# Router choices by a maximum and index of eight, and first-stage scatters issued in two groups

## The reference

```python
x = x + 0.5 * ffn(layernorm(x))       # 16 experts, the best 2 of each token
x = x + attn(layernorm(x))            # 16 heads, 4 key/value heads, causal
x = x + 0.5 * ffn(layernorm(x))

def ffn(x):
    probs = softmax(x @ router_w)                    # 256 x 16
    routing_weights, routing_idx = top_k(probs, 2)
    routing_weights /= sum(routing_weights)
    # every chosen expert: silu(x @ gate) * (x @ up) @ down, summed with the weights
```

## Time and profile before

| what | us |
|---|---|
| median of 3 runs (858.55 to 863.77) | 861.68 |
| span of the profiled execution | 874.5 |
| the profiled execution's own time | not given apart from its span |
| pool 0 and 1 routed, experts of pool 0 begin | 39.6 |
| experts of pool 1 begin | 87.3 |
| attention runs at PE's pace from about | 222 |

### The profile page before, as it was taken

How to read it: one execution, slowest core, us unless ns; L and a number is a source line. 1 busy time by engine, 2 the same in 40 slices (tenths; PEclk the granted TensorE clock), 3 DMA queues, 4 the chain that set the end, 5 groups by cost and what they waited for, 6 DMA issues and landing times.

```text
span 874.5 us, 16309 instructions
## 1 busy us (share of the span) xinstructions
PE 778.9 (89%) x4584; PEld 667.8 (76%) x4584; DVE 656.2 (75%) x1823; ACT 582.4 (67%) x1538; POOL 451.7 (52%) x410
## 2 busy tenths in 40 slices
PE   3678999899999999999999999999988887899980
PEld 3567878678778888888888887888877777787770
DVE  6645575568988888889988889987899877675463
ACT  2335666687777878877878787787765665554540
POOL 1466232488465866575656655455442782003354
PEclk9789899999999999999999999999999999999995
DMA  9478983212000110000000000000000165256675
GB/s 296 131 213 272 246 243 119 82 22 31 1 1 8 18 19 7 1 13 13 2 13 13 1 1 1 1 2 1 8 0 1 43 220 168 79 160 195 204 210 180
DMA packets 53207, 70.91 MB, mean 81 GB/s; under 512 B 7296, under 2 KB 44928, under 8 KB 52736
## 3 DMA queue, kind: packets, MB, share of 16 engines
q1 hardware_dynamic: 41024, 47.80, 18.1%
q0 software_dynamic: 9216, 16.82, 7.8%
q10 hardware_dynamic: 2880, 5.24, 2.0%
HBM read 42.80 MB, written 27.03 MB: 80 GB/s over the span
## 4 chain that ended last, share of the span: by engine, by line
PE 59%; issue 12%; POOL 11%; DVE 10%; DMA 3%; ACT 2%; SPq 1%; POOLq 0%; DVEq 0%; ACTq 0%
PE ps L1694 49%; PE ps L1891 5%; POOL sb_ropeB L1639 2%; POOL sb_xf L1642 2%; PE ps L1749 2%; POOL xs L1608 1%; POOL sb_x L1630 1%; POOL sb_wF L1650 1%; POOL xs L1601 1%; DVE sb_x L1488 1%; PE ps L1763 1%; DMA xs<-sb_rowC,sb_toC 1%; PE ps L1711 1%; DVE sb_prob L1461 1%; DMA sb_work<-xs 1%
## 5 line engine op out<-in xcount | busy, mean ns | idle before, releaser
L1694 PE MATMUL ps<-sb_wF 128*128 128x512 f32 (+2 forms) x1056 | 262.0, 375 | 9.3 <-DVE sb_wF L1478 6.8
L1694 PEld LDWEIGHTS ps<-sb_wF 128*128 128x128 f32 x1056 | 173.4, 191 | 28.6 <-issue 8.7
L1020 ACT ACTIVATE sb_prob<-sb_prob,sb_nmax 128x128 f32<-128x128 f32 (+3 forms) x256 | 142.2, 559 | 43.8 <-DVE sb_nmax L1461 40.3
L1639 POOL TENSOR_TENSOR sb_ropeB<-sb_ropeB,sb_sin 128x512 f32<-128x512 f32 x80 | 110.9, 1386 | 106.5 <-ACT sb_ropeB L1001 106.4
L1694 PE MATMUL ps<-sb_wF,sb_wA 128*128 128x512 f32 x576 | 154.9, 404 | 6.3 <-ACT sb_ropeB L1001 5.7
L1650 POOL TENSOR_TENSOR sb_wF<-sb_xf,sb_wF 128x384 fp32r<-128x384 f32 (+1 forms) x75 | 82.0, 1101 | 121.0 <-ACT sb_wF L1013 120.8
L1488 DVE SCALAR_TENSOR_TENSOR sb_x<-ps,sb_rinv,sb_x 128x256 f32<-128x256 f32 x256 | 122.5, 479 | 23.3 <-PE ps L1694 9.8
L1694 PEld LDWEIGHTS ps<-sb_wF,sb_wA 128*128 128x128 f32 x576 | 102.2, 188 | 32.0 <-ACT sb_ropeB L1001 13.1
L1694 PE MATMUL ps<-sb_wA,sb_wF 128*128 128x256 f32 x768 | 116.1, 287 | 10.0 <-DVE sb_x L1488 7.1
L1468 DVE TENSOR_TENSOR sb_wF<-ps,sb_wF 128x512 fp32r<-128x512 f32 x160 | 109.2, 684 | 19.7 <-ACT sb_wF L1029 17.1
L1029 ACT ACTIVATE sb_wF<-ps 128x512 fp32r<-128x512 f32 x160 | 95.3, 596 | 42.9 <-PE ps L1891 42.3
(11 more groups left out here) (203 smaller groups left out, 1320.7 us busy)
## 6 DMA issues: line engine op xcount, KB each, us to landing
ys<-sb_wA_raw SPq DMA_DIRECT2D x124, 128.0 KB
sb_wF_raw<-xs SPq DMA_DIRECT2D x44, 128.5 KB
sb_wA_raw<-xs SPq DMA_DIRECT2D x44, 128.5 KB
sb_work<-xs SPq DMA_DIRECT2D x36, 128.5 KB
sb_wA_raw<-in_wattn ACTq DMA_DIRECT2D x18, 256.0 KB, 3.4
sb_wF_raw<-in_wgu SPq DMA_DIRECT2D x4, 768.0 KB
sb_wF_raw<-in_wdn SPq DMA_DIRECT2D x4, 768.0 KB
sb_wA_raw<-in_wgu SPq DMA_DIRECT2D x4, 768.0 KB
```

Of the source, the lines that this page charges most:

```text
L1020: nc.scalar.activation(own, own, ACT.Exp, scale=-1.0, bias=nmax[:, k % 2, h:h + 1], accum_out=ssum[:, k % 2, h:h + 1]).then_inc(exp_done, 1)
L1639: nc.gpsimd.tensor_tensor(ropeB[:, slot], ropeB[:, slot], sin[:], ALU.mult).then_inc(rope_mul, 1)
L1694: return nc.tensor.matmul(out, lhsT, rhs, start=start, stop=stop)
```

## The change

Four things change. **The choice of experts:** for each row of tokens one maximum-of-eight instruction gives the eight largest logits and one index-of-eight instruction their positions, so the two chosen experts and the gap are read off. For the two pools of the first mixture and for the last pool both read the logits in PSUM, and their copy to SBUF falls away; pool 2 still copies. A pool of 12 rows thus has 24 small instructions; two comparisons then make the tables of the choices, laid out expert by expert where they were row by row. In pool 1 the logits of the first 8 rows are in another bank than those of the last 4, and the first 8 are searched by themselves, then the last 4. **Rows 8 to 11 of pool 1** are normalised by VectorE, not ACT. **The first mixture's scatters** go out as all the firsts of a pool, then in two halves one copy of weights and that half's seconds (`scatter_parts`); the wait for pool 0's results is gone. **Pool 1's tables and gather places** are made in five pieces in steps 3, 5, 7, 9 and 11 of pool 0's experts, not two in steps 2 and 4.

```diff
+    FIRST_HALVES, ACT_ROWS = 4, 8
...
-    LEAD, PACED = 9, 13
...
         lx_copy(pools[1], 0)
         for j in (4, 5):
             normalise(pools[1], j)
-        for h in range(1, pools[1].nh):
+        lx_copy(pools[1], 1)
+        for j in (6, 7):
+            normalise(pools[1], j)
+        for h in range(2, pools[1].nh):
             lx_copy(pools[1], h)
-            for j in range(2 * h + 4, min(2 * h + 6, pools[1].nt)):
-                normalise(pools[1], j)
...
-        def pick_top(q, m):
-            link(nc.vector.tensor_reduce(per_token(q, "lm", m), plane(q, 0), AX_X, ALU.max))
-            link(nc.vector.tensor_tensor(plane(q, 1), plane(q, 0), over_e(q, per_token(q, "lm", m)), ALU.is_ge))
-
-        def pick_first(q):
-            rev = falling(q).rearrange("p (o e) -> p o e", o=1).broadcast_to([P, plane(q, 1).shape[1], E])
-            link(nc.vector.tensor_tensor(plane(q, 1), plane(q, 1), rev, ALU.mult))
-            link(nc.vector.tensor_reduce(per_token(q, "lm", 2), plane(q, 1), AX_X, ALU.max))
-
-        def pick_out(q, k):
-            link(nc.vector.tensor_tensor(plane(q, 2 + k), plane(q, 1), over_e(q, per_token(q, "lm", 2)), ALU.is_ge))
...
+        def find_top(q, first, last):
+
+            if q.p == 2:
+                dve.wait_ge(lcopy_done, copies(q, last // 2 - 1))
+            else:
+                dve.wait_ge(logit_done, q.halves + (last // 2 if q.p == 1 else q.nh))
+            for t in range(first, last):
+                step(nc.vector.max(top_value(q, t), logit_row(q, t)))
+            settle()
+            for t in range(first, last):
+                ins = nc.vector.max_index(top_index(q, t), top_value(q, t), logit_row(q, t))
...
+        def pick(q, k):
+
+            a = rising(q).rearrange("p (e o) -> p e o", o=1).broadcast_to([P, E, q.nt])
+            b = index_of(q, k).rearrange("p (o t) -> p o t", o=1).broadcast_to([P, E, q.nt])
+            step(nc.vector.tensor_tensor(plane(q, 2 + k), a, b, ALU.is_equal))
...
-                if q.p == 0 and i in (2, 4):
-
-                    places(pools[1], 3 + (i == 4))
+                if q.p == 0 and i in (3, 5, 7):
+                    tables(pools[1], (i - 3) // 2)
+                elif q.p == 0 and i in (9, 11):
+                    move(pools[1], (i - 9) // 2)
...
-        lcopy(pools[0], 0)
-        for part in range(7):
-            if part == 3:
-                second_norm()
+        route(pools[0], 0)
+        route(pools[0], 1)
+        route(pools[0], 3)
+        second_norm()
+        for part in (4, 5, 6):
             route(pools[0], part)
         shares(pools[0])
-        for part in range(5):
+        for part in range(3):
             places(pools[0], part)
-        lcopy(pools[1], 0)
-        for part in range(7):
+        rows(pools[1], ACT_ROWS, pools[1].nt)
+        for part in (3, 4):
+            places(pools[0], part)
+        find_top(pools[1], 0, 2 * FIRST_HALVES)
+        find_top(pools[1], 2 * FIRST_HALVES, pools[1].nt)
+        for part in (3, 4, 5, 6):
             route(pools[1], part)
...
-            if q.p == 1 and 2 * n > LEAD:
-
-                pool.wait_ge(y_evac, min(2 * n - LEAD, PACED))
...
+        def scatter_parts(q):
+
+            parts = (range(0, q.nt // 2), range(q.nt // 2, q.nt))
+            pool.wait_ge(to_done, q.p + 1)
+            pool.wait_ge(weight_done, q.p + 1)
+            for part, rows in enumerate(parts):
+                for t in rows:
...
+                    nc.gpsimd.indirect_dma_start(out=xs[q.p][:], out_offset=place_of(q, 0, t), in_=rows_of(q)[:, t],
+                                                 in_offset=None).then_inc(first_in[2 * q.p + part], 16)
+            for part, rows in enumerate(parts):
+                pool.wait_ge(first_in[2 * q.p + part], 16 * len(rows))
+                own = slice(rows.start, rows.stop)
+                nc.gpsimd.tensor_copy(row_weights(q)[:, own], wgt[:, q.t0 + rows.start:q.t0 + rows.stop]).then_inc(second_set, 1)
+                pool.wait_ge(second_set, 2 * q.p + part + 1)
+                for t in rows:
+                    nc.gpsimd.indirect_dma_start(out=xs[q.p][:], out_offset=place_of(q, 1, t), in_=rows_of(q)[:, t],
+                                                 in_offset=None).then_inc(scattered[q.p], 16)
...
         for q in pools[0:2]:
-            for n in range(q.nt + SECOND):
-                scatter(q, n)
+            scatter_parts(q)
```

More of the change, by code:

```diff
@@ L10 @@
 I32 = mybir.dt.int32
+U32 = mybir.dt.uint32
 ALU = mybir.AluOpType
@@ L170, in program @@
     RING, XR, FR, GR = 8, 10, 4, 16
+    PART_ROWS = [q.nt // 2 for q in pools[0:2] for _ in range(2)]
     w_in = [sem(f"w_in{n}") for n in range(2)]
@@ L1170, in pick_first @@
-        def pick_first(q):
-            rev = falling(q).rearrange("p (o e) -> p o e", o=1).broadcast_to([P, plane(q, 1).shape[1], E])
-            link(nc.vector.tensor_tensor(plane(q, 1), plane(q, 1), rev, ALU.mult))
-            link(nc.vector.tensor_reduce(per_token(q, "lm", 2), plane(q, 1), AX_X, ALU.max))
-        def pick_out(q, k):
-            link(nc.vector.tensor_tensor(plane(q, 2 + k), plane(q, 1), over_e(q, per_token(q, "lm", 2)), ALU.is_ge))
-        def route(q, part):
-            if part == 0:
-                dve.wait_ge(lcopy_done, copies(q, span(q)[1] // 2 - 1))
-                dve.wait_ge(cf_in, 16 * (1 if q.p < 2 else q.p))
[L1183 to L1192, removed]
+            dve.wait_ge(logit_done, q.halves + h + 1)
@@ new lines, in lcopy @@
+            nc.vector.tensor_copy(ROUTE[q.p]["L"][:, 2 * h * E:2 * (h + 1) * E], logits_at(q, h)).then_inc(lcopy_done, 1)
+        def find_top(q, first, last):
+            if q.p == 2:
+                dve.wait_ge(lcopy_done, copies(q, last // 2 - 1))
[6 more added lines that the diff above has]
+                ins = nc.vector.max_index(top_index(q, t), top_value(q, t), logit_row(q, t))
+                if q.p != 2 and t == q.nt - 1:
+                    ins.then_inc(lcopy_done, 1)
+                    dve.wait_ge(lcopy_done, copies(q, 0))
+                else:
+                    step(ins)
@@ L1193, in route @@
             elif part == 5:
[L1194 to L1197, removed]
+                pick(q, 1)
             else:
@@ L1231, in places, with tables @@
             elif part == 3:
+                for piece in range(3):
+                    tables(q, piece)
+            else:
+                for k in range(2):
+                    move(q, k)
+        def tables(q, piece):
+            r = ROUTE[q.p]
+            te, end, base, scratch, count, first, back = (r["ex"][:, i] for i in range(7))
+            if piece == 0:
                 link(nc.vector.tensor_scalar(r["exi"][:, 0], count, float(P - 1), None, ALU.add))
@@ L1235, in places @@
                 link(nc.vector.tensor_tensor_scan(end, te, te, 0.0, ALU.add, ALU.max))
+            elif piece == 1:
                 link(nc.vector.tensor_tensor(base, end, te, ALU.subtract))
@@ L1247, in places, with move @@
                   .then_inc(begin_done, 1)
-            else:
-                for k in range(2):
-                    moved = per_token(q, "lm", 2)
-                    link(nc.vector.tensor_tensor(plane(q, 1), plane(q, 2 + k),
-                                                 back.rearrange("p (o e) -> p o e", o=1).broadcast_to([P, q.nt, E]),
-                                                 ALU.mult))
-                    link(nc.vector.tensor_reduce(moved, plane(q, 1), AX_X, ALU.add))
-                    link(nc.vector.tensor_tensor(r["pf"][:, k, 0:q.nt], r["pf"][:, k, 0:q.nt], moved, ALU.subtract))
+        def move(q, k):
+            r = ROUTE[q.p]
+            back, moved = r["ex"][:, 6], per_token(q, "lm", 2)
+            link(nc.vector.tensor_tensor(plane(q, 1), plane(q, 2 + k),
+                                         back.rearrange("p (e o) -> p e o", o=1).broadcast_to([P, E, q.nt]), ALU.mult))
+            link(nc.vector.tensor_reduce(moved, turned(plane(q, 1)), AX_X, ALU.add))
+            link(nc.vector.tensor_tensor(r["pf"][:, k, 0:q.nt], r["pf"][:, k, 0:q.nt], moved, ALU.subtract))
+            if k == 1:
                 nc.vector.tensor_copy(pos[:, :, q.t0:q.t0 + q.nt], r["pf"][:, :, 0:q.nt]).then_inc(pos_done, 1)
@@ L1701, in logit_transposes @@
             at = q.halves + h
-            pe.wait_ge(xn_done[q.p], 2 * h + 2)
+            if q.p == 1 and 2 * h >= ACT_ROWS:
+                pe.wait_ge(xn_done[0], pools[0].nt + 2 * h + 2 - ACT_ROWS)
+            else:
+                pe.wait_ge(xn_done[q.p], 2 * h + 2)
             if q.p == 2:
```

83 lines of the change are left out of this document (47 added, 36 removed).

## The result

The changed kernel takes 852.19 us (median of 4 runs, 851.05 to 853.58), the kernel before on the same chip 862.26 (858.55 to 863.77): a ratio of 0.9888, 95% interval 0.9861 to 0.9915, so 10.1 us faster. The prediction was 854.0 in a range of 847 to 864. The profiled execution took 852.63, its span is 850.8.

What follows compares the result with a forecast made beforehand. Pool 1's late first tile load was taken to hold the first mixture, and VectorE to set the pace late in attention. From 861.7, 6.5 (first mixture) and 1.3 (pool 2) came off: 854 us, range 847 to 864.

Steps and rivals of the forecast that it cites:

- pool 3's choice: Last pool's choice of experts, in fixed steps of pool 2's experts: hidden by their matmuls, gain nothing; without that cover about 1.
- Part 1: Pool 1's choice on VectorE: maximum 0.11, index 0.20, first 8 rows hidden beside PE; gain 3.2, between 0.6 and 3.6.
- Part 2: Pool 0: shorter choice gains nothing before its first scatter, but its experts begin 1.4 earlier; lower bound 0.4.
- Part 3: Pool 1's scatters: POOL starts at 39.9, last issue 70.1, first tile at 75.8, with no waits for results.
- Part 4: Pool 1's tables in five pieces no longer hold up PE at 50.49: gain 1.5, or nothing if pieces still delay a result.
- The pause: PE's 4.51 standstill at 52.17, without a found cause; the forecast leaned to its absence from the runs, first tile 5.1 sooner.
- Part 5: Pool 2's choice inside attention: 8.4 becomes 5.9, half counted, gain 1.3; from a loss of 1.7 to a gain of 3.6.
- Dear instructions: Rival: maximum 0.22 and index 0.44, so pool 1's choice gains only 0.6; 860 us; chance 0.12.
- Starved tiles: Rival: unpaced scatters take DMA rate from pool 0's loads, PE runs dry, 14 lost against 8 gained; 868 us; chance 0.13.
- Shared losses: Rival: pool 1's tile comes early, but part of the scatter traffic slows the loads; 858 to 865 us; chance 0.10.
- Pause in every run: Rival: PE's standstill belongs to all runs, so the full 9.6 and 1.3 to 3 are gained; 849 to 851; chance 0.17.

Runs made afterwards that it cites:

- before_again: The kernel before, with no edit, profiled once more: one run, 861.88 us, span 860.1.
- groups_alone: The kernel before with only the grouped, unpaced scatters of pools 0 and 1, all choices of experts old: 858.46 us, ratio 0.9971.
- after: The changed kernel as first measured and profiled, against the kernel before: 852.19 us, ratio 0.9888.
- rows_by_act: The changed kernel with ScalarE (ACT) normalising all twelve tiles of pool 1's rows, none left to VectorE: 851.85 us.
- after_again: The changed kernel with no edit, timed and profiled once more beside its variants: 852.56 us.
- old_scatters: The changed kernel with pools 0 and 1's scatters in the old interleaved order, pool 1's paced by evacuated tiles: 855.53 us.
- choice_twice_third: The changed kernel with pool 2's search (maximum and index, twelve tiles of rows) done twice: 855.86 us.
- old_choice_third: The changed kernel with the old choice of experts for pool 2 alone: 856.90 us.
- combined: The changed kernel with all pool 1 rows normalised by ScalarE, pool 0's tanh and ranks earlier, and begin taken off the places once in the moves: 852.31 us.

## Why the prediction was right, and where it was not

**The time** came out 1.8 below the forecast: 10.1 us were gained where 7.8 were forecast (6.5 and 1.3). What the forecast lacks lies in pool 2, which gave 4.5. For the first mixture 10.1 less 4.5 leaves 5.6; its end in before_again against the two profiles of the changed kernel gives 6.0 to 6.8. So its 6.5 can't be told from what was measured. If it was 5.6, some of the closeness of the total is luck: 0.9 too much in one term against 3.2 too little in the other. The attention part in single profiles of the old choice is 2.8 to 5.3 longer, with 4.5 in groups_alone. Undone one at a time, the parts cost 3.0 (scatters), 1.9 (choice of pools 0 and 1), 4.5 (choice of pool 2) and at most 1.1 (pieces): 9.4 to 10.5 of the 10.1. From the second mark to the end it is 118.3 in before_again and 118.6 in after: pool 3's choice gave nothing, as forecast.

**Part 1, pool 1's choice.** The prices hold: 0.09 for a maximum (0.11 taken), 0.15 for an index (0.20). The rule of the Trainium skill that spoke against the change, "VectorE: DVE Perf Modes", TRN2 errata, is not borne out here: by the prediction's estimate from it a row would take 0.42, and it took 0.26 (3.1 for twelve). The first eight rows were not hidden beside PE, since VectorE came to them only at 28.09: it had four rows to normalise and pool 0's tables to make. From the end of PE's last logits to the end of the scan it is 6.4 in before_again (30.4 to 36.8), 4.1 in after (29.2 to 33.3) and 3.4 in rows_by_act (28.7 to 32.1): 2.3 gained where 3.2 was forecast, and 3.0 with the four rows left to ScalarE. Undoing the choice of pools 0 and 1 costs 1.9; POOL's start moves by 2.3 there.

**Part 2.** The experts' first transposes stand at 38.01, 38.2 was forecast. But before_again has them at 38.68, not 39.59, and after_again at 37.21, so how much was gained here can't be read from one pair of profiles: 0.7 to 1.5 against before_again.

**Part 3.** POOL starts at 37.31 and issues last at 67.19, 2.6 and 2.9 sooner than forecast. Most of this is the profile that the forecast started from: in before_again POOL starts at 41.32, 2.1 sooner than in the earlier trace rows. The landing took 4.78 and the load after it 2.66 (72.12 to 74.78), so that it was 7.6 from issue to tile, not the 5.7 taken from the earlier trace rows; two errors that nearly cancel bring the tile to 74.78 for 75.8. The order and the missing wait together are worth 3.0 (old_scatters), 2.5 to 3.3 without the rest (groups_alone): the largest piece of the first mixture. Without the pause it is the order that counts, as far as before_again tells, since POOL then waits for no result.

**Part 4.** Right in the mechanism, the stall; worth at most 1.1 and perhaps nothing, since the stall that falls is mostly replaced by waits for tiles.

**The pause.** Taking it for one execution's own, mostly, was right: before_again has none. The forecast without it has the tile 5.1 sooner, and it came 5.2 to 5.7 sooner (80.01 in before_again against 74.78 and 74.33).

**Part 5, pool 2: the term that was mis-sized**, outside its own bounds (a loss of 1.7 to a gain of 3.6). VectorE's saving was about right, 2.5 forecast and 2.2 measured: the 14 old instructions take 8.83 and the new search with its five followers 6.6. The step that failed is "PE is busy too (7.5 of 10), so I take half". With VectorE above 9 of 10 about all of it counts: choice_twice_third shows 3.3 for 3.1. That the old choice costs more than its VectorE time, 4.5, goes with PE's waits and the clock of 0.83 after them; that these make up the rest was seen in the trace and not isolated by a run.

**Rivals.** Dear instructions: refuted by the rows of the search. Starved tiles: PE is full at 350 to 365 GB/s, and the paced order is slower. Shared losses: the time is below its 858, though landing and load took 1.9 longer than in the earlier trace rows. Pause in every run: refuted, though the time it gave is near.

What stays open: why the clock rises at different times in executions that do the same up to there; and the slope of the first mixture for a start of POOL much later than 39.6.

## What to carry to other kernels

Where one engine is above 9 of 10 in a stretch, start from the full time of an instruction saved on it, as choice_twice_third shows it here, and expect more where its lateness lets TensorE pause; do not halve it because TensorE looks busy as well. A transfer that releases the next stage is paced by its last issue: put the issues in the order that ends soonest, and read ahead of it whether the engine idles before the first. Profile the kernel before twice before pricing a pause that the trace has no name for.

## What the runs showed of the hardware

Some short VectorE instructions last until GpSimd's are done; the maximum and the index don't. VectorE's timeline in after, then POOL's:

```profile
627.85 0.39 DVE L1179 MAX8 sb_lgC<-sb_LC 128x8 f32<-128x16 f32 x4
...
628.65 0.17 DVE L1182 FIND_INDEX8 sb_lgC<-sb_lgC,sb_LC 128x8 uint32<-128x16 f32 x1
...
630.40 0.17 DVE L1202 TENSOR_TENSOR sb_lmC<-sb_lgC 128x12 f32<-128x12 f32 x1
...
662.83 1.81 DVE L1280 TENSOR_TENSOR sb_pfC<-sb_pfC,sb_lmC 128x12 f32<-128x12 f32 x1
```

```profile
627.13 1.28 POOL L1688 TENSOR_TENSOR sb_ropeB<-sb_ropeB,sb_sin 128x512 f32<-128x512 f32 x1 [0.21 <-ACT sb_ropeB L1016]
628.48 1.31 POOL L1691 TENSOR_TENSOR sb_xf<-sb_xf,sb_ropeB 128x512 f32<-128x512 f32 x1
...
662.21 1.07 POOL L1628 DMA_INDIRECT xs<-sb_rowC,sb_toC  x1 [0.17 <-issue]
663.32 1.29 POOL L1688 TENSOR_TENSOR sb_ropeB<-sb_ropeB,sb_sin 128x512 f32<-128x512 f32 x1
```

The same shape of 128x12 takes 0.17 while POOL is idle and 1.81 where it ends with POOL's product (664.64 and 664.61). Four maxima beside POOL take their usual 0.39, an index its 0.17. The Trainium skill, "SBUF — State Buffer", section "SBUF: two separate sides", says that GpSimd and a VectorE instruction with two SBUF inputs, or in a mode that uses two ports, share one pair of ports: whichever comes first holds it and the other blocks. The rows of old_choice_third agree: 629.75 begins within POOL's product of 629.58 and lasts until 0.22 after its end. The row of 1.81 agrees in part only: it ends with POOL's product but begins 0.49 before it, while POOL issues a scatter (662.21, 1.07), and no run shows why it didn't come first. In combined the wait stands at another instruction with two inputs. So, as far as the rows show it, a part of what the new choice is worth inside attention is that its search does not wait for GpSimd: of the old choice's 8.83, some 3.2 is stretch (0.93, 1.34, 1.06 and 1.14 for what takes about 0.36, 0.36, 0.36 and 0.17 without it), of the new one's 6.6 some 1.5, nearly all in the addition (0.76) and the scan (1.50), which stayed.
